# Graph network layer: one-hots by two-input 16-bit compares on interleaved tables, and 10 count rows for the first tile

## The reference

```
# layer 0
m   = silu(concat(x[src], x[dst], edge) @ mW1 + mb1) @ mW2 + mb2
agg = segment_sum(m, dst)
x   = layernorm(x + (layernorm(x + mlp(concat(x, agg))) * gamma + beta))
# layer 1
agg = segment_sum(x[src], dst) / max(deg, 1)
x   = layernorm(x + relu(relu(concat(x, agg) @ W1 + b1) @ W2 + b2))
```

## Time and profile before

| | us |
|---|---|
| median of 3 runs | 2572.13 |
| lowest and highest | 2570.74, 2573.39 |
| span of the profiled execution, first to last instruction | 2569.7 |

### The profile page before, as it was taken

The page is one execution under the profiler, slowest core; times in us unless marked ns, Lnnn a source line. Parts: engine busy times, 40 slices in busy tenths (PEclk is TensorE's granted clock), DMA queues, the critical chain, the costliest instruction groups (busy, mean ns, idle before and its releaser), DMA issues. The chain is left out here.

```text
span 2569.7 us, 58924 instructions
## 1 busy us (share of the span) xinstructions
PE 2182.9 (85%) x21030; PEld 1871.4 (73%) x21030; DVE 1577.3 (61%) x4059; ACT 847.9 (33%) x1368; POOL 1664.2 (65%) x1618
## 2 busy tenths in 40 slices
PE   7898888888888988898889888988898878799996
PEld 7786777677777776776777776767677754699994
DVE  4786676667666766676667666766676647600005
ACT  3343333333333433333333333333333326200004
POOL 4777777777777777777777777777777755200002
PEclk9899999899899989998899999999999988899998
DMA  6555545554555555545554555455545543688871
GB/s 236 197 190 190 167 159 185 181 169 154 177 190 173 158 180 181 187 141 180 184 190 139 186 175 190 144 182 176 191 150 176 176 118 96 245 309 302 303 268 51
DMA packets 135225, 471.71 MB, mean 184 GB/s; under 512 B 55730, under 2 KB 77490, under 8 KB 113555
## 3 DMA queue, kind: packets, MB, share of 16 engines
q1 hardware_dynamic: 84586, 368.35, 41.1%
q0 software_dynamic: 50176, 102.86, 14.3%
q10 hardware_dynamic: 426, 0.03, 0.0%
HBM read 369.41 MB, written 101.70 MB: 183 GB/s over the span
## 5 line engine op out<-in xcount | busy, mean ns | idle before, releaser
L519 POOL DMA_INDIRECT gath<-P_d,src_i x1540 | 1543.2, 1002 | 469.4 <-issue 465.5
L650 PE MATMUL ps_pre<-wc,eT 128*128 128x128 f32 x3136 | 702.4, 306 | 13.7 <-DVE counts L567 13.7
L682 PE MATMUL ps_sum<-h,edgeN 128*128 128x129 f32 x3136 | 486.2, 302 | 265.7 <-ACT h L744 265.2
L590 DVE TENSOR_TENSOR pre<-ps_pre,gath 128x512 f32<-128x512 f32 x392 | 265.9, 678 | 588.6 <-issue 548.7
L682 PEld LDWEIGHTS ps_sum<-h,edgeN 128*128 128x128 f32 x3136 | 422.2, 209 | 278.1 <-ACT h L744 277.7
L744 ACT ACTIVATE h<-pre 128x512 f32<-128x512 f32 x392 | 247.9, 632 | 1122.2 <-DVE pre L590 1068.3
L666 PE MATMUL ps_cnt<-edgeK,edgeL 128*128 128x500 bf16 (+1 forms) x3136 | 585.1, 336 | 29.6 <-DVE edgeK L580 29.4
L580 DVE TENSOR_SCALAR edgeK<-iota,key 128x600 bf16<-128x600 f16 (+2 forms) x1568 | 526.4, 396 | 0.0
L652 PE MATMUL ps_pre<-Qw,nodeE 128*128 128x128 bf16 x4704 | 520.4, 220 | 0.0
L650 PEld LDWEIGHTS ps_pre<-wc,eT 128*128 128x128 f32 x3136 | 478.1, 192 | 32.6 <-issue 29.6
L666 PEld LDWEIGHTS ps_cnt<-edgeK,edgeL 128*128 128x128 bf16 x3136 | 320.1, 105 | 199.3 <-DVE edgeK L580 42.8
(11 more groups left out here) (128 smaller groups left out, 1021.4 us busy)
## 6 DMA issues: line engine op xcount, KB each, us to landing
eT<-eT SPq DMA_DIRECT2D x56, 1792.0 KB, 9.2
A_d<-counts SPq DMA_DIRECT2D x56, 1568.0 KB
A_c<-A_d SPq DMA_DIRECT2D x56, 1568.0 KB, 8.1
rel_b<-rel_d SPq DMA_DIRECT2D x56, 896.0 KB
gath<-P_d,src_i POOLq DMA_INDIRECT x1568
Qw<-Q_d SPq DMA_DIRECT2D x56, 96.0 KB
Q_d<-Qst SPq DMA_DIRECT2D x7, 672.0 KB, 7.8
xT_sb<-xT SPq DMA_DIRECT2D x7, 448.0 KB, 8.1
```

What stands on the lines that cost most here:

```text
L519: pool.indirect_dma_start(gath[:, q, t * D:(t + 1) * D], None, v["P_d"], bass.IndirectOffsetOnAxis(ap=src_i[k][:, c:c + 1], axis=0)).then_ ...
L590: V.tensor_tensor(pre[x][:], ps_pre[x][:], gath[:, q, :], ALU.add).then_inc(pre_add, 1)
L650: T.matmul(o, eT[k][:, e0:e0 + P], wc[:], start=True, stop=False)
L682: last = T.matmul(ps_sum[k][:, 0:SW], edgeN[x][:, t, :], h[x][:, t, 0:SW], start=(q == 0 and t == 0), stop=(q == GQ - 1 and t == QT - 1))
```

## The change

`edgeL`, `edgeK` and `nodeE` are now made by `tensor_tensor` compares in which both inputs and the output have 2-byte elements. To this end the keys `low` and `key` are stored as 16-bit floats, the tables are written out in full on GpSimd once at the start, and tables and one-hots are laid out with the tile as the innermost index: `edgeL` has the four tiles' columns interleaved (step of 4 elements between one tile's columns), and `edgeK` has two tiles interleaved in each of two tensors (step of 2 elements). The compare for `nodeE` gets its second input from a table `pidE` of 256 columns that holds the partition's number and is read seven times in a row. `edgeN` stays a compare with 32-bit keys and output. The window of the first tile goes from 20 rows to 10, so the count has 10, 10, 12 and 12 rows; the condition that the inputs must meet for this path (each tile's destinations lie in its window) follows the same table.

```diff
@@ -35,11 +35,11 @@
 NW = NP_ + P
 SPREAD = -(-(EP - N_EDGES) // (NP_ - N_NODES))
 W0 = 20
-WIN = [(0, W0), (2, 10), (5, 12), (8, 12)]
+WIN = [(0, 10), (2, 10), (5, 12), (8, 12)]
 AB = 25
 A2 = 2 * AB
-ROFF = [A2 * sum(w for _, w in WIN[:j]) for j in range(QT)]
-RCOLS = ROFF[-1] + A2 * WIN[-1][1]
+PAIRS = [(j, WIN[j][1]) for j in range(0, QT, 2)]
+PE_ = 256
 GW = 120
 LASTQ = P - W0
 CLEARED = 96
@@ -83,7 +83,10 @@
         ident = sb("ident", [P, P])
         identb = sb("identb", [P, P], BF16)
         pid = sb("pid", [P, 1])
-        iota = sb("iota", [P, 1000], F16)
+        iota = sb("iota", [P, P], F16)
+        iotaL = sb("iotaL", [P, P, QT], F16)
+        iotaK = [sb(f"iotaK{j}", [P, A2 * w, 2], F16) for j, w in PAIRS]
+        pidE = sb("pidE", [P, PE_], BF16)
         wc = sb("wc", [P, D])
         eps_col = sb("eps_col", [P, 1])
...
     def gpsimd(pool):
         pool.iota(pid[:], [[0, 1]], base=0, channel_multiplier=1, allow_small_or_imprecise_dtypes=True).then_inc(made, 1)
-        pool.iota(iota[:], [[1, 1000]], base=0, channel_multiplier=0, allow_small_or_imprecise_dtypes=True).then_inc(made, 1)
+        pool.iota(iota[:], [[1, P]], base=0, channel_multiplier=0, allow_small_or_imprecise_dtypes=True).then_inc(made, 1)
...
         pool.memset(zeros[:], 0.0).then_inc(made, 1)
@@ -232,6 +236,11 @@
         for m in (ident, identb):
             pool.affine_select(out=m[:], in_=m[:], compare_op=ALU.not_equal, fill=1.0, base=0,
                                pattern=[[-1, P]], channel_multiplier=1).then_inc(made, 1)
+        pool.iota(iotaL[:], [[1, P], [0, QT]], base=0, channel_multiplier=0, allow_small_or_imprecise_dtypes=True)
+        for t, (j, w) in zip(iotaK, PAIRS):
+            pool.iota(t[:], [[1, A2 * w], [WIN[j + 1][0] - WIN[j][0], 2]], base=WIN[j][0], channel_multiplier=0,
+                      allow_small_or_imprecise_dtypes=True)
+        pool.iota(pidE[:], [[0, PE_]], base=0, channel_multiplier=1, allow_small_or_imprecise_dtypes=True).then_inc(made, 1)
...
     def settled(eng):
 
-        eng.wait_ge(made, 8)
+        eng.wait_ge(made, 9)
...
-    key = [sb(f"key{k}", [P, GT]) for k in range(2)]
-    low = [sb(f"low{k}", [P, GT]) for k in range(2)]
+    key = [sb(f"key{k}", [P, GT], F16) for k in range(2)]
+    low = [sb(f"low{k}", [P, GT], F16) for k in range(2)]
     edgeN = [sb(f"edgeN{k}", [P, QT, P]) for k in range(2)]
-    edgeL = [sb(f"edgeL{k}", [P, QT, P], BF16) for k in range(2)]
-    edgeK = [sb(f"edgeK{k}", [P, RCOLS], BF16) for k in range(2)]
+    edgeL = [sb(f"edgeL{k}", [P, P, QT], BF16) for k in range(2)]
+    edgeK = [[sb(f"edgeK{k}{j}", [P, A2 * w, 2], BF16) for j, w in PAIRS] for k in range(2)]
...
@@ -550,7 +560,9 @@
                 V.scalar_tensor_tensor(kq[:, :, j], bq[:, :, j], float(w), rq[:, :, j], ALU.mult, ALU.add)
 
         def expand(k, cols):
-            return V.tensor_scalar(nodeE[k][:, cols], rel_b[:, cols], pid[:, 0:1], None, ALU.is_equal)
+            part = lambda t: t[:, cols].rearrange("p (a b) -> p a b", b=PE_)
+            same = pidE[:].unsqueeze(1).broadcast_to([P, (cols.stop - cols.start) // PE_, PE_])
+            return V.tensor_tensor(part(nodeE[k]), part(rel_b), same, ALU.is_equal)
...
@@ -575,10 +587,10 @@
             c = slice(q * QT, (q + 1) * QT)
             io = iota[:, 0:P].unsqueeze(1).broadcast_to([P, QT, P])
             V.tensor_tensor(edgeN[x][:], io, rel_g[k][:, c].unsqueeze(2).broadcast_to([P, QT, P]), ALU.is_equal)
-            V.tensor_tensor(edgeL[x][:], io, low[k][:, c].unsqueeze(2).broadcast_to([P, QT, P]), ALU.is_equal)
-            for j, (w0, w) in enumerate(WIN):
-                last = V.tensor_scalar(edgeK[x][:, ROFF[j]:ROFF[j] + A2 * w], iota[:, w0:w0 + A2 * w],
-                                       key[k][:, q * QT + j:q * QT + j + 1], None, ALU.is_equal)
+            V.tensor_tensor(edgeL[x][:], iotaL[:], low[k][:, c].unsqueeze(1).broadcast_to([P, P, QT]), ALU.is_equal)
+            for to, io, (j, w) in zip(edgeK[x], iotaK, PAIRS):
+                two = key[k][:, q * QT + j:q * QT + j + 2].unsqueeze(1).broadcast_to([P, A2 * w, 2])
+                last = V.tensor_tensor(to[:], io[:], two, ALU.is_equal)
             last.then_inc(onehots, 1)
...
@@ -662,15 +674,15 @@
             for b in range(2):
                 o = ps_cnt[x][:, b, 0:AB * W0].rearrange("p (a d) -> p a d", d=W0)
                 for j, (w0, w) in enumerate(WIN):
-                    r = edgeK[x][:, ROFF[j] + b * AB * w:ROFF[j] + (b + 1) * AB * w].rearrange("p (a d) -> p a d", d=w)
-                    last = T.matmul(o[:, :, w0:w0 + w], edgeL[x][:, j, :], r, start=(j == 0),
-                                    stop=(j == QT - 1 and q == 0))
+                    r = edgeK[x][j // 2][:, b * AB * w:(b + 1) * AB * w, j % 2].rearrange("p (a d) -> p a d", d=w)
+                    last = T.matmul(o[:, :, w0:w0 + w], edgeL[x][:, :, j], r, start=(j == 0),
+                                    stop=(j == QT - 1 and q == 0), skip_group_check=True)
             if q > 0:
                 pe.wait_ge(carried, g * (GQ - 1) + q)
                 for b in range(2):
                     o = ps_cnt[x][:, b, 0:AB * W0].rearrange("p (a d) -> p a d", d=W0)
                     last = T.matmul(o[:, :, 0:1], identb[:], carry[x][:, b * AB:(b + 1) * AB].unsqueeze(2),
-                                    start=False, stop=True)
+                                    start=False, stop=True, skip_group_check=True)
```

More of the change, by code:

```diff
@@ L147, in build_prepare @@
     pid, ident, identb, iota = v["pid"], v["ident"], v["identb"], v["iota"]
+    iotaL, iotaK, pidE = v["iotaL"], v["iotaK"], v["pidE"]
     flag, offs, gbase = v["flag"], v["offs"], v["gbase"]
@@ L411, in build_edges @@
     flag, offs, gbase, force_general = v["flag"], v["offs"], v["gbase"], v["force_general"]
-    pid, ident, identb, iota, wc = v["pid"], v["ident"], v["identb"], v["iota"], v["wc"]
+    ident, identb, iota, wc = v["ident"], v["identb"], v["iota"], v["wc"]
+    iotaL, iotaK, pidE = v["iotaL"], v["iotaK"], v["pidE"]
     sumT, deg = v["sumT"], v["deg"]
```

## The result

| | before | after |
|---|---|---|
| median of four runs, us | 2572.76 | 2669.02 |
| lowest and highest | 2570.74, 2574.09 | 2664.18, 2670.18 |
| span of the profiled execution | 2569.7 | 2667.6 |

The account below looks back on a forecast made before the run. GpSimd's chain of gap plus gather (1.307 us, 1540 times, 2013 us) was taken to bound the edge loop. GpSimd +70, start 0, all else hidden: 2572.1 + 70 = 2642 us, range 2520 to 2720.

Parts of the forecast that it names:

- two thirds of the way from 21 to 97 us: GpSimd's added gather loss, placed between the results of the first rate (97) and the second rate (21): +70 us.
- the first rate: Gather loss if only `edgeN` and `edgeL` hold gathers today: 141 us per us² of hold, 97 us more than now.
- Rivals 3 and 4: New compares: 3, half pace not reached, about 2900 us, 8%; 4, one-input pace of 0.30 ns, about 2560 us, 3%.
- Rival 1: 16-bit compares on VectorE hold no gather, only `edgeN` is left with 44 us instead of 88: 2528 us, 12%.
- rival 2: Two-input compares hold nothing and `tensor_scalar` was the cause, so all 88 us would go: 2484 us, 2%.
- neighbours share a hold: In the gather chain, a held gather shifts the next one; taken to lean back from the first rate, no size of its own.
- One-input compares hardly hold: Reading of old `edgeK`: a gather starting 0.61 us into its four `tensor_scalar` compares was held only 0.07 us.
- the second rate: Gather loss if `tensor_scalar` compares hold in full too: 82 us per us² of hold, 21 us more than now.
- the prediction's own 0.36 us²: Sum of squared holds for old `edgeK`, if its four one-input compares held in full, about 0.30 us each.
- the bounds of 0.47 and 1.03 us: TensorE, worst cost per quad of `edgeL`'s stepped weight loads (+0.47) and of stepped moving operands (+1.03); taken as zero.
- Rival 5: TensorE becomes the bound of the edge loop at 5.73 us a quad, +190 us: 2765 us, 4%.
- Rival 6: Gathers pass the short gaps between compares regularly, making one hold of 2.1 us: some 2950 us, 2%.

Follow-up runs that it names:

- the faster version: The changed kernel with only `edgeK` made by four one-input compares again; 2537.37 us, 0.9879 of the kernel before.
- the kernels of 1067 to 1123 ns: The kernel before with `edgeN`, or `edgeN` and `edgeL`, by four one-input compares each, the latter also with 10 rows for the first tile; ratios 1.0122, 1.0141, 1.0115, 1.0103.

## Why the prediction was right, and where its size was off

**The bound.** Right. GpSimd's chain was the bound before, after, and in the faster version: gap 0.305 each time, idle time "issue". 1540 x (0.305 + 1.066) = 2111 us is the loop of 2109.

**The pace of the new compares.** Right. The two forms of `edgeK` give (774 - 671)/200 = 0.52 ns per element, the value taken; durations 420, 671, 774 and 1082 ns against 410, 670, 770 and 1080 forecast. Rivals 3 and 4 (full pace, one-input pace) fall. The Trainium skill (VectorE: DVE Perf Modes, the perf-mode tier table) has this half pace for `tensor_tensor` on bf16 in SBUF, and these rows agree. Here the inputs of `edgeL` and `edgeK` are 16-bit floats of another kind (f16), and the second operand is read in rows of 2 or 4 elements that repeat; the pace is the same.

**16-bit two-input compares hold gathers.** Right: all 377 starts in the new `edgeK` that fall between the first 0.08 and the last 0.06 us of a compare were held. Rival 1 (no holds) falls with them, and so does rival 2 (two-input compares hold nothing and `tensor_scalar` was the cause).

**The size: the mis-sized term.** The step that put the loss two thirds of the way from 21 to 97 us was wrong; it was 97, the end of the first rate. But the agreement is of the sum, not of its parts, and is luck. At the first rate, brought to the longer quad (187/1.38 = 135 us per us²), the terms should be `edgeN` 42, `edgeL` 11, `edgeK` 97, `nodeE` 35. They are 56, 12, 114 and 6.

The rule takes starts as spread evenly over the quad, and they are not. A gather that `edgeN` has held starts its successor 0.55 + 1.25 = 1.80 us behind `edgeN`'s start. In the kernel before that is the last 0.11 us of `edgeK`'s second compare: 148 of the 157 successors are there, and they are most of the 201 starts in it, each held 0.06. In the changed kernel it is 0.28 us into the second long one: 202 of 203, most of the 252 starts held 0.37. `nodeE` lies where few gathers start, 13 in place of the 1540 x 2/7 x 0.96/5.48 = 77 of an even spread. In the version with `edgeK` by one-input compares 67 start in it, and 62 of these in its last 0.06 us, unheld, although it is a two-input compare. I had named the effect ("neighbours share a hold") and let it pull the sum down; here it pushed it up.

**One-input compares hardly hold.** Wrong as a reading. The first rate charges nothing for `tensor_scalar`, and the count by line seems to bear it out with 12 us of the 88 before. But the gather of the earlier trace rows that I took as its sign does not show it, once the compares are taken one by one:

```profile
1018.10 0.33 DVE L580 TENSOR_SCALAR edgeK<-iota,key 128x500 bf16<-128x500 f16 x1
1018.35 0.37 DVE L580 TENSOR_SCALAR edgeK<-iota,key 128x600 bf16<-128x600 f16 x1
```

It started at 1018.24, 0.14 us into the second compare, and was held to 1018.24 + 1.01 - 0.94 = 1018.31, 0.04 before the next one: a full hold, of which only 0.07 was left. All 201 starts at this place were held so; of the other 200, 186 fell into the last 0.06 us of a compare, where nothing is left to wait for, and 12 right at a compare's start. So the second rate's premise (one-input compares hold in full) was the better one, and what the trace refutes in both rates is the even spread: with the prediction's own 0.36 us² it would charge 147 x 0.36 = 53 us to the old `edgeK`, where 12 were lost. Only close behind a compare's start may the forms differ: in the table above none of the 51 starts in the first 0.08 us of a one-input compare was held, and 37 of the 68 in two-input ones were. Why gathers sit through whole rows of short compares in the kernels of 1067 to 1123 ns stays open; all of those ran where the gathers were not the bound.

**TensorE.** Right as to the path. The first tile's matmuls fell from 405 to 296 ns, but TensorE's busy time only by 34 us. Weight loads took 119 in place of 104 ns, and 250 columns 296 in place of 287; that is 8 x 15 ns of loads and 4 x 9 ns of matmuls in a quad, far from the bounds of 0.47 and 1.03 us, and over 390 quads it would account for the 58 us missing from 92 if none of it were hidden. The loads go with the step of `edgeL`: in the version with `edgeK` by one-input compares, where `edgeL` keeps its step and `edgeK` has none, they take 119 ns too, and 250 columns take 291. Rival 5 (TensorE as the bound) falls with GpSimd's 7 us of waiting.

**The start and the cheaper VectorE.** Worth nothing, as said: the loop's first gather starts at 82.5 against 82.6, and VectorE's 56 us less of work turned into waiting. Rival 6 (gathers that pass the gaps between compares) was not what happened in the changed kernel: 6 gathers of 1540 are over 0.7 us too long. On the chips with the longer times it is real: 15 to 49 of them with 25 to 92 us in the kernels that keep `edgeN` in two-input form.

## What to carry to other kernels

Where GpSimd issues indirect DMAs one after another and never waits, read their mean against their median: the difference times the count is what another engine costs them, and the line that ran on VectorE at each start names it. Making VectorE faster was worth nothing here; the lengths of its instructions, and where the gathers met them, were worth -34 and +97 us. Shortening a compare by 2-byte operands helped (`edgeL`, 36 to 12 us), merging four short ones into two long ones did not (`edgeK`, 12 to 114). A count of small holds beside one kind of instruction does not show that it holds nothing: look how much of the instruction was left when the others started.

A loop whose stages are held and then released at fixed distances is not met evenly. Before using an average over phases, work out where the successor of a held instruction starts.

## What the runs showed of the hardware that was not expected

- The kernel before took 2572 and 2573 us in two groups of runs and 3075, 3121, 3121 and 3122 in four others, steady within 1% in each. In the longer ones matmuls of the same form last longer (L650 338 ns in the kernel with 10 rows, 305 in the kernel before) and TensorE stands before them for nothing named. The order of kernels need not be the same on both: the changed kernel with `nodeE` by one-input compares is at 0.9942 of the kernel before there. The cause is open.
- A one-input compare holds a gather like a two-input one (201 of 203 and 43 of 46 starts in the middle of `edgeK`'s); in both forms the gather is let go some 0.05 us before VectorE's next instruction starts.
- A gather can be held through seven one-input compares, until 1.51 us after its start, and can pass unheld beside the same kind (40 of 104 starts).
- Splitting a two-input compare in two did not halve what gathers lose in it (77 to between 61 and 65 us), and gathers that start in the compare ahead of it lose more (10 to between 30 and 52 us).
